# A gated feed-forward kernel: the closing addition of the gate moved from GpSimd to VectorE

## The chip, the cores and the metric

The kernel runs on one core of a Trainium2 chip. The metric is the time of one execution on the device in microseconds, as the median of several runs. The engines are called as in the profile: PE (TensorE), DVE (VectorE), ACT (ScalarE), POOL (GpSimd), SP (SyncE, which issues the DMAs).

## The reference

For each of 8 batches of 512 rows and 512 columns, with FF = 2048:

```python
scale = cond @ norm_w.T + 1.0
ms = jnp.mean(x * x, axis=-1, keepdims=True)
h = x * (scale[:, None, :] * jax.lax.rsqrt(ms + EPS))
u = h @ up_w.T
val, gate = jnp.split(u, 2, axis=-1)
h = val * jax.nn.gelu(gate, approximate=False)
hq = act_quant(h)        # round(h * 127 / max|h| of the row), clipped, scaled back
wq = weight_quant(down_w)  # -1, 0, 1 times a scale from mean|down_w|
y = hq @ wq.T + x
```

## The kernel before

The up-projection is done transposed: features on the partitions, the 512 rows of a batch (T) on the free axis. The 2048 features are cut into 16 slices of 128 (FT = 16). For one slice the value and the gate, each split into two halves of H = 256 rows, are made by seven block products in Winograd's form of Strassen's scheme instead of eight. Each product is six matmuls (two halves of the contraction; the operands are split into a high and a low float16 part and three of the four combinations are summed). The stretch in which PE makes the seven products of slice s is called slot s here. PE issues them in the order p1(s), p5(s), p4(s-1), p6(s), p3(s), p2(s), p7(s): p4, which closes the first half of the gate, belongs to the slice before.

PE accumulates in two pairs of banks (A0/A1, B0/B1), which ACT copies out in between ("snapshots"):

- line 571, `snap_u3`: the sum of p1, p6, p7 of slice s, from bank A into the left half of `snapC`; after it PE may add p4(s) to the bank (line 1019 waits for it), and the bank then holds the first half of the gate.
- lines 576 and 584, `snap_p1` and `snap_u2`, into `snapPU`; line 580, `snap_p5`, from bank B into the right half of `snapC`.
- line 475, `gate_second`: the left half of `snapC` plus its right half. This is the second half of the gate. It is the step that the change moves.
- line 589, `gelu_first`, reads bank A; line 594, `gelu_second`, reads `snapC` and waits for `gate_second`.

ACT's queue in slot s is snap_u3(s-1), snap_p1(s), snap_p5(s), gelu_first(s-1), snap_u2(s), gelu_second(s-1), and then a piece of the work for the next batch (`x_ahead`: squares in slots 2 and 3, `x_out` (line 551) in slots 6, 7, 10, 11, `x_high` (line 557) in slots 8, 9, 12, 13).

DVE's queue in slot s of a batch b is, before the change: in slot 1 `quant_scale` (788 to 796) for batch b-1; in slot 4 `rms`; in slot 5 `refine` (693 to 699) and `normalise` (704) for batch b+1; in slots 9, 10, 13, 14 `x_low` (720); in slots 2 to 9 the three steps `q_scale`, `q_round`, `q_clip` (801, 806, 811) that quantise two slices of batch b-1; `staged_out` (826) after each down-projection; then hidden(s-1) (767: value times c times gelu), value(s) (761) and, after slices 1, 5, 8, 11, 14, 15, `largest` (780, 784), which takes the row maximum over the slices since the last. The one in slot 6, after slice 5, reduces four slices. After slice 15 it completes `m`, which PE transposes in slot 1 (line 1043) for `quant_scale`.

PE makes the down-projection of batch b-1 (line 1055, 16 matmuls per tile of 128 rows) after slots 10, 12, 13 and 14 of batch b.

Batches 2 to 6 are one loop body. Batch 0 also prepares the weights: `w_scale` (DVE, 726 to 735) finds the scale of slice s+2 in slot s, `w_mix` (POOL, 456 to 468) forms the combinations of its blocks, PE transposes them in slot s+1 (983), ACT and DVE write their high and low parts (567 and 741) into `wslots`; slices from 4 on are stored to DRAM and read back in every later batch. Batch 1 also rounds `down_w` (`down_clip` on POOL, 493 and 496; `down_round` on DVE, 848). POOL's queue in later batches holds the addition, `rsqrt` in slot 4 (448) and `x_mix` in slots 8 and 12 (482 to 487).

All order is written by hand, with one semaphore per kind of step; each engine works through its queue in order.

```python
            def gelu_second(b, s):
                act.wait_ge(gate2_ready, FT * b + (s + 1))
...
            def p4(b, s):
                pe.wait_ge(u3_snap, FT * b + (s + 1))
```

Of the kernel before, what the change touches and what calls it, by code (L numbers as in the profile page):

```python
# [23 lines left out]
def gated_ffn_program(nc, x, cond, norm_w, up_w, down_w, out):  # L24
# [4 lines left out]
    B, T, D = x.shape  # L29
# [80 lines left out]
    with ctx:  # L110
# [324 lines left out]
        @block.gpsimd  # L435
        def _(pool):
            pool.memset(ident[:, :], 0.0).then_inc(ident_steps, 1)
            pool.memset(ones[:, :], 1.0)
            pool.memset(neg_half[:, :], -0.5)
            pool.wait_ge(ident_steps, 1)  # L440
            pool.affine_select(out=ident[:, :], in_=ident[:, :], compare_op=ALU.not_equal, fill=1.0,
                               base=0, pattern=[[-1, P]], channel_multiplier=1).then_inc(ident_steps, 1)
            pool.wait_ge(ident_steps, 2)
            pool.tensor_copy(ident16[:, :], ident[:, :]).then_inc(consts_ready, 1)

            def rsqrt(b):
                pool.wait_ge(ms_ready, b + 1)
                pool.tensor_tensor(r_pow[:, :], ms[:, :], neg_half[:, :], ALU.pow).then_inc(pow_ready, 1)

            def w_mix(p):  # L450
                f = wf(p)
                done = MIX * p
                pool.wait_ge(w_scale_ready, p + 1)
                if p >= 2:
                    pool.wait_ge(wT_psum, NC * (p - 1))
                pool.tensor_scalar(f[:, A21:A22 + 1, :].rearrange("p a n -> p (a n)"), wst[:, p % WSTAGE, 1, :],
                                   inv_w[:, VG * p + 1:VG * p + 2], 1.0, ALU.mult, ALU.mult).then_inc(mix_steps, 1)
                pool.tensor_scalar(f[:, A11:A12 + 1:A12 - A11, :],
                                   wst[:, p % WSTAGE, 0, :].rearrange("p (a n) -> p a n", a=2),
                                   inv_w[:, VG * p:VG * p + 1], 1.0, ALU.mult, ALU.mult).then_inc(mix_steps, 1)  # L460
                pool.wait_ge(mix_steps, done + 1)
                pool.tensor_tensor(f[:, S1, :], f[:, A21, :], f[:, A22, :], ALU.add).then_inc(mix_steps, 1)
                pool.wait_ge(mix_steps, done + 2)
                pool.tensor_tensor(f[:, S3, :], f[:, A11, :], f[:, A21, :], ALU.subtract).then_inc(mix_steps, 1)
                pool.wait_ge(mix_steps, done + 3)
                pool.tensor_tensor(f[:, S2, :], f[:, S1, :], f[:, A11, :], ALU.subtract).then_inc(mix_steps, 1)
                pool.wait_ge(mix_steps, done + 5)
                pool.tensor_tensor(f[:, S4, :], f[:, A12, :], f[:, S2, :], ALU.subtract).then_inc(mix_steps, 1)

            def gate_second(b, s):  # L470

                n = FT * b + (s + 1)
                pool.wait_ge(u3_snap, n)
                pool.wait_ge(p5_snap, n)
                pool.tensor_tensor(snapC[:, s % 2, 0:H], snapC[:, s % 2, 0:H], snapC[:, s % 2, H:T], ALU.add)\  # L475
                    .then_inc(gate2_ready, 1)

            def x_mix(b, kp):
                f = xf_of(b, kp).rearrange("p (a t) -> p a t", a=NB)
                done = 8 * b + 4 * kp  # L480
                pool.wait_ge(xf_ready, KT * b + (2 * kp + 2))
                pool.tensor_tensor(f[:, T3, :], f[:, B22, :], f[:, B12, :], ALU.subtract).then_inc(xmix_steps, 1)
                pool.tensor_tensor(f[:, T1, :], f[:, B12, :], f[:, B11, :], ALU.subtract).then_inc(xmix_steps, 1)
                pool.wait_ge(xmix_steps, done + 2)
                pool.tensor_tensor(f[:, T2, :], f[:, B22, :], f[:, T1, :], ALU.subtract).then_inc(xmix_steps, 1)
                pool.wait_ge(xmix_steps, done + 3)
                pool.tensor_tensor(f[:, T4, :], f[:, B21, :], f[:, T2, :], ALU.subtract).then_inc(xmix_steps, 1)

            def down_clip(i):

                pool.wait_ge(dw_loaded[i % 2], 16 * (PIECES // 2 + i // 2 + 1))
                pool.wait_ge(dw_scale_ready, 1)
                pool.tensor_scalar(dwb[:, i % 2, :], dwb[:, i % 2, :], sw[:, 0:1], MAGIC, ALU.mult, ALU.add)\
                    .then_inc(dw_added, 1)
                pool.wait_ge(dw_added, i + 1)
                pool.tensor_scalar(dwb[:, i % 2, :], dwb[:, i % 2, :], MAGIC + 1.0, MAGIC - 1.0, ALU.min, ALU.max)\
                    .then_inc(dw_clipped, 1)

            def batch(b, first=False, final=False):
                for s in range(FT):  # L500
                    gate_second(b if s else b - 1, (s - 1) % FT)
                    if not final:
                        if s == RMS_AT:
                            rsqrt(b + 1)
                        if s in XMIX_AT:
                            x_mix(b + 1, XMIX_AT[s])
                    if first and s in DW_CLIP:
                        down_clip(DW_CLIP[s])

            w_mix(0)  # L510
            rsqrt(0)
            w_mix(1)
            for s in range(FT):
                if s > 0:
                    gate_second(0, s - 1)
                if s + 2 < FT:
                    w_mix(s + 2)
                if s == RMS_AT:
                    rsqrt(1)
                if s in XMIX_AT:  # L520
                    x_mix(1, XMIX_AT[s])
            batch(1, first=True)
            with pool.Fori(2, LAST) as b:
                batch(b)
            batch(LAST, final=True)
            gate_second(LAST, FT - 1)

        @block.scalar
        def _(act):
# [156 lines left out]
        def _(dve):  # L686
# [62 lines left out]
            def c_later():  # L749
                c_rest = c_all[:, FT * VC:B * FT * VC].rearrange("p (b n v) -> p b n v", b=LAST, v=VC)  # L750
                for v, of in enumerate((0, 1, 1)):
                    dve.tensor_tensor(c_rest[:, :, :, v],
                                      c_w[:, of:FT * VG:VG].unsqueeze(1).to_broadcast([P, LAST, FT]),
                                      c_b[:, 1:B].unsqueeze(2).to_broadcast([P, LAST, FT]), ALU.mult).then_inc(c_ready, 1)

            def value(b, s):

                n = FT * b + (s + 1)
                dve.wait_ge(val_psum, n)
                dve.wait_ge(u2_snap, n)  # L760
                dve.tensor_tensor(h_tile(b, s), BB[s % 2][:, :], snapPU[:, s % 2, :], ALU.add).then_inc(val_ready, 1)  # L761

            def hidden(b, s):
                n = FT * b + (s + 1)
                dve.wait_ge(gelu2_done, n)
                dve.wait_ge(val_ready, n)
                dve.scalar_tensor_tensor(out=h_tile(b, s), in0=h_tile(b, s), scalar=c_of(b, s, 0), in1=g[:, s % 2, :],  # L767
                                         op0=ALU.mult, op1=ALU.mult).then_inc(h_ready, 1)
# [80 lines left out]

            def batch(b, first=False, final=False):  # L850
                for s in range(FT):
                    if s == 1:
                        quant_scale(b - 1)
                        if first:
                            dve.wait_ge(dw_steps, 3)
                    if not final:
                        if s == RMS_AT:
                            rms(b + 1)
                        if s == REFINE_AT:
                            refine(b + 1)  # L860
                            normalise(b + 1)
                        if s in XLO_AT:
                            x_low(b + 1, *divmod(XLO_AT[s], 2), XLO_AT[s] + 1)
                    if 0 <= s - QUANT_FROM < PAIRS:
                        q_scale(b - 1, s - QUANT_FROM)
                        q_round(b - 1, s - QUANT_FROM)
                        q_clip(b - 1, s - QUANT_FROM)
                    if not final and s - 1 in DOWN_AFTER:
                        staged_out(b - 1, DOWN_AFTER[s - 1])
                    of, before = (b, s - 1) if s else (b - 1, FT - 1)  # L870
                    hidden(of, before)
                    value(b, s)
                    largest(of, before)
                    if first and s in DW_TERN:
                        down_round(DW_TERN[s])
# [40 lines left out]

            for s in range(FT):
                if s > 0:
                    value(0, s - 1)
                    if s + 2 < FT:  # L920
                        w_scale(s + 2)
# [21 lines left out]
            with dve.Fori(2, LAST) as b:  # L943
                batch(b)
            batch(LAST, final=True)
            hidden(LAST, FT - 1)
            largest(LAST, FT - 1)
            quant_scale(LAST)
# [246 lines left out]
```

## Time and profile before

| | us |
|---|---|
| median of 3 runs | 823.17 (820.63 to 823.93) |
| the profiled execution | 822.39 |
| its span | 820.6 |
| PE busy | 770.3 |
| DVE busy | 616.1 |
| ACT busy | 428.6 |
| POOL busy | 250.9 |
| the moved addition (line 475), 128 times | 101.1 in sum, 0.79 mean |

The granted TensorE clock over the span is 0.989 of full speed. PE's rows name matmuls by line and operand; a matmul of the up-projection lasts 0.27 us in the records and the next starts 0.11 us later, since they are pipelined. The same holds on DVE and ACT to a lesser degree: an independent next instruction starts up to 0.1 us before the recorded end of the one before. In a timeline the columns are the start, the duration, the engine, the line, the operation with what it writes and reads, and, in brackets, the idle time before it with the step that ended it.

### The profile page before, as it was taken

The numbers are of one execution on the slowest core, as the hardware profiler recorded it, in microseconds if no ns is written. First come the engines' busy times: TensorE is split into PE (matmuls) and PEld (weight loads), VectorE is DVE, ScalarE is ACT, GpSimd is POOL, SyncE is SP. The second block draws the span as 40 slices with busy tenths as digits, with TensorE's granted clock in tenths as the row PEclk, the third lists the DMA queues.
The fourth block names the chain that finished last, engine by engine and source line by source line (L and its number), as shares of the span: only waits on it lengthen the run. The fifth ranks groups of instructions, "written<-read, shape, count | busy, mean of one in ns | idle before, by whom it ended". The sixth has DMA issues, their size and how long they took to land.

```text
span 820.6 us, 17515 instructions
## 1 busy us (share of the span) xinstructions
PE 770.3 (94%) x6385; PEld 636.2 (78%) x6385; DVE 616.1 (75%) x890; ACT 428.6 (52%) x997; POOL 250.9 (31%) x313
## 2 busy tenths in 40 slices
PE   5788887987999999999999999999999999999987
PEld 4677776875778897789878887789868987888853
DVE  5889798889854896389846895489657994589577
ACT  4677565564544664355543654355535654445523
POOL 4477777343421232112221232123211232111100
PEclk9999999999999999999999999999999999999999
DMA  4546662745455255443456154535545245505512
GB/s 142 208 133 205 192 213 119 295 156 166 177 184 184 65 197 182 136 173 134 149 179 228 53 194 142 187 114 179 170 163 179 94 175 185 186 32 195 187 52 77
DMA packets 34507, 130.88 MB, mean 159 GB/s; under 512 B 3224, under 2 KB 3744, under 8 KB 34464
## 3 DMA queue, kind: packets, MB, share of 16 engines
q1 hardware_dynamic: 34448, 130.30, 47.1%
q8 instruction: 27, 0.44, 0.2%
q14 instruction: 16, 0.13, 0.1%
q10 hardware_dynamic: 16, 0.00, 0.0%
HBM read 110.89 MB, written 19.40 MB: 159 GB/s over the span
## 4 chain that ended last, share of the span: by engine, by line
PE 73%; DVE 5%; DMA 2%; issue 1%; POOL 1%; ACT 1%; SPq 0%; DVEq 0%; POOLq 0%; ACTq 0%
PE A L1003 11%; PE A L1006 11%; PE A L1005 11%; PE Y L1055 11%; PE B L1006 8%; PE B L1003 8%; PE B L1005 8%; DMA xin<-in_x_dram 2%; DVE h L801 1%; PE X L971 1%; DMA dwb<-in_L_cond_down_w_dram 1%; PE X L1043 1%; DVE h L816 0%; DVE mpart L780 0%; DVE wst L848 0%
## 5 line engine op out<-in xcount | busy, mean ns | idle before, releaser
L1003 PE MATMUL A<-xT,wslots 128*128 (+1 forms) x1024 | 282.2, 276 | 14.8 <-ACT snapC L571 8.5
L1005 PE MATMUL A<-xT,wslots 128*128 (+1 forms) x1024 | 282.2, 276 | 0.0
L1006 PE MATMUL A<-xT,wslots 128*128 (+1 forms) x1024 | 282.1, 275 | 0.0
L475 POOL TENSOR_TENSOR snapC<-snapC 128x256 f32<-128x256 f32 x128 | 101.1, 790 | 463.5 <-ACT snapC L571 462.9
L1005 PE MATMUL B<-xT,wslots 128*128 (+1 forms) x768 | 210.2, 274 | 0.0
L1003 PE MATMUL B<-xT,wslots 128*128 (+1 forms) x768 | 210.2, 274 | 0.0
L1006 PE MATMUL B<-xT,wslots 128*128 (+1 forms) x768 | 210.2, 274 | 0.0
L767 DVE SCALAR_TENSOR_TENSOR h<-h,c_all,g 128x512 f32<-128x512 f32 (+1 forms) x128 | 108.3, 846 | 118.7 <-ACT g L594 117.9
L1003 PEld LDWEIGHTS A<-xT,wslots 128*128 128x128 f16 x1024 | 101.2, 99 | 30.9 <-ACT snapC L571 9.8
L1005 PEld LDWEIGHTS A<-xT,wslots 128*128 128x128 f16 x1024 | 101.2, 99 | 15.1
L1006 PEld LDWEIGHTS A<-xT,wslots 128*128 128x128 f16 x1024 | 101.3, 99 | 12.7
L1055 PE MATMUL Y<-dT,q 128*128 128x512 f16 x448 | 101.3, 379 | 2.1 <-DVE wst L826 2.1
L576 ACT ACTIVATE snapPU<-A 128x256 f32<-128x256 f32 x128 | 49.2, 384 | 97.4 <-PE A L1006 97.4
L571 ACT ACTIVATE snapC<-A 128x256 f32<-128x256 f32 x128 | 49.0, 383 | 95.0 <-PE A L1006 94.9
L761 DVE TENSOR_TENSOR h<-B,snapPU 128x512 f32<-128x512 f32 (+1 forms) x128 | 87.4, 683 | 1.2 <-PE B L1006 1.0
L589 ACT ACTIVATE g<-A,c_all 128x256 f32<-128x256 f32 x128 | 60.6, 473 | 46.7 <-PE A L1006 42.8
L1006 PEld LDWEIGHTS B<-xT,wslots 128*128 128x128 f16 x768 | 75.5, 98 | 9.0
L1005 PEld LDWEIGHTS B<-xT,wslots 128*128 128x128 f16 x768 | 75.5, 98 | 8.8
L1003 PEld LDWEIGHTS B<-xT,wslots 128*128 128x128 f16 x768 | 75.5, 98 | 8.4
L1055 PEld LDWEIGHTS Y<-dT,q 128*128 128x128 f16 x448 | 43.8, 98 | 49.1 <-issue 2.3
L780 DVE TENSOR_REDUCE mpart<-h 128x512 f32<-128x1536 f32 (+2 forms) x40 | 81.0, 2025 | 0.2
L801 DVE TENSOR_TENSOR h<-h,S 128x1024 f32<-128x1024 f32 x64 | 77.5, 1211 | 0.7 <-PE S L1049 0.7
(128 smaller groups left out, 920.1 us busy)
## 6 DMA issues: line engine op xcount, KB each, us to landing
wslots<-w_scratch SPq DMA_DIRECT2D x84, 896.0 KB, 4.7
w_scratch<-wslots SPq DMA_DIRECT2D x12, 896.0 KB, 4.6
wst<-in_L_cond_up_w_dram SPq DMA_DIRECT2D x16, 512.0 KB, 6.2
xin<-in_x_dram SPq DMA_DIRECT2D x8, 1024.0 KB, 7.3
dwb<-in_L_cond_down_w_dram SPq DMA_DIRECT2D x16, 512.0 KB, 4.5
wst<-in_x_dram SPq DMA_DIRECT2D x28, 256.0 KB, 5.4
out_dram<-wst SPq DMA_DIRECT2D x28, 256.0 KB, 5.2
xin<-in_x_dram SPq DMA_DIRECT2D x4, 256.0 KB, 5.1
```

What stands on the lines that cost most here:

```text
L475: pool.tensor_tensor(snapC[:, s % 2, 0:H], snapC[:, s % 2, 0:H], snapC[:, s % 2, H:T], ALU.add)\
L571: act.activation(snapC[:, s % 2, 0:H], BA[s % 2][:, 0:H], ACT.Copy).then_inc(u3_snap, 1)
L576: act.activation(snapPU[:, s % 2, 0:H], BA[s % 2][:, 0:H], ACT.Copy).then_inc(p1_snap, 1)
L589: act.activation(g[:, s % 2, 0:H], BA[s % 2][:, 0:H], ACT.Gelu, scale=c_of(b, s, 1))\
L761: dve.tensor_tensor(h_tile(b, s), BB[s % 2][:, :], snapPU[:, s % 2, :], ALU.add).then_inc(val_ready, 1)
L767: dve.scalar_tensor_tensor(out=h_tile(b, s), in0=h_tile(b, s), scalar=c_of(b, s, 0), in1=g[:, s % 2, :], op0=ALU.mult, op1=ALU.mult).then_ ...
L780: dve.tensor_reduce(into[:, :], h_tiles(b, first, n).rearrange("p n t -> p t n"), AX.X, ALU.max, apply_absolute_value=True).then_inc(max_r ...
L801: dve.tensor_tensor(pair, pair, S[:, :].unsqueeze(1).to_broadcast([P, 2, T]), ALU.mult)\
L1003: pe.matmul(into, high, xh, start=(start and kp == 0), stop=False, skip_group_check=not start)
L1005: pe.matmul(into, high, xl, start=False, stop=False, skip_group_check=not start)
L1006: mm = pe.matmul(into, low, xh, start=False, stop=last, skip_group_check=not start)
L1055: mm = pe.matmul(bank[:, :], of[:, s * T + t * P:s * T + (t + 1) * P], dT[:, s, :], start=(s == first), stop=(s == last))
```

## The change

The additions leave POOL's queue and stand in DVE's. In slot s, gate_second(s-1) is now the first thing in DVE's queue, ahead of everything listed above; in batch 0 it stands ahead of value(s-1) and w_scale(s+2). It waits for the same two snapshots and signals the same semaphore. Nothing else changes.

```diff
-            def gate_second(b, s):
-
-                n = FT * b + (s + 1)
-                pool.wait_ge(u3_snap, n)
-                pool.wait_ge(p5_snap, n)
-                pool.tensor_tensor(snapC[:, s % 2, 0:H], snapC[:, s % 2, 0:H], snapC[:, s % 2, H:T], ALU.add)\
-                    .then_inc(gate2_ready, 1)
-
...
                 for s in range(FT):
-                    gate_second(b if s else b - 1, (s - 1) % FT)
                     if not final:
...
             for s in range(FT):
-                if s > 0:
-                    gate_second(0, s - 1)
                 if s + 2 < FT:
...
             batch(LAST, final=True)
-            gate_second(LAST, FT - 1)
 
...
+            def gate_second(b, s):
+
+                n = FT * b + (s + 1)
+                dve.wait_ge(u3_snap, n)
+                dve.wait_ge(p5_snap, n)
+                dve.tensor_tensor(snapC[:, s % 2, 0:H], snapC[:, s % 2, 0:H], snapC[:, s % 2, H:T], ALU.add)\
+                    .then_inc(gate2_ready, 1)
+
...
                 for s in range(FT):
+                    gate_second(b if s else b - 1, (s - 1) % FT)
                     if s == 1:
                         quant_scale(b - 1)
...
                 if s > 0:
+                    gate_second(0, s - 1)
                     value(0, s - 1)
                     if s + 2 < FT:
                         w_scale(s + 2)
...
             batch(LAST, final=True)
+            gate_second(LAST, FT - 1)
             hidden(LAST, FT - 1)
```

DVE's queue in the loop body (batches 2 to 6), from hidden(5) in slot 6 to value(7) in slot 7, before:

```order
L767 SCALAR_TENSOR_TENSOR h<-h,c_all,g 128x512
L759 REGISTER_ALU
L761 TENSOR_TENSOR h<-B,snapPU 128x512 [waits u2_snap,val_psum]
L780 TENSOR_REDUCE mpart<-h 128x512 [waits h_ready]
L783 ISA
L784 TENSOR_TENSOR m<-m,mpart 128x512 [waits max_ready]
L801 TENSOR_TENSOR h<-h,S 128x1024 [waits qscale_psum]
```

and with the change, where the same steps have the lines 763, 757, 776, 780 and 797:

```order
L763 SCALAR_TENSOR_TENSOR h<-h,c_all,g 128x512
L755 REGISTER_ALU
L757 TENSOR_TENSOR h<-B,snapPU 128x512 [waits u2_snap,val_psum]
L776 TENSOR_REDUCE mpart<-h 128x512 [waits h_ready]
L779 ISA
L780 TENSOR_TENSOR m<-m,mpart 128x512 [waits max_ready]
L749 TENSOR_TENSOR snapC<-snapC 128x256 [waits p5_snap,u3_snap]
L797 TENSOR_TENSOR h<-h,S 128x1024 [waits qscale_psum]
```

The addition (line 749) stands behind the reduction over four slices and its maximum, and ahead of q_scale.

DVE's queue in batch 0, from the last low parts of a slice's weights to the scale of a later slice, before:

```order
L741 TENSOR_TENSOR wslots<-S,wslots 128x256 [waits whi_ready]
L761 TENSOR_TENSOR h<-B,snapPU 128x512 [waits u2_snap,val_psum]
L726 TENSOR_REDUCE inv_w<-wst 128x2 [waits w_loaded2]
L729 TENSOR_SCALAR c_w<-inv_w 128x2 [waits w_steps]
L732 TENSOR_SCALAR c_w<-c_w 128x2 [waits w_steps]
L735 RECIPROCAL inv_w<-c_w 128x2 [waits w_steps]
```

and with the change:

```order
L729 TENSOR_TENSOR wslots<-S,wslots 128x256 [waits whi_ready]
L749 TENSOR_TENSOR snapC<-snapC 128x256 [waits p5_snap,u3_snap]
L757 TENSOR_TENSOR h<-B,snapPU 128x512 [waits u2_snap,val_psum]
L714 TENSOR_REDUCE inv_w<-wst 128x2 [waits w_loaded2]
L717 TENSOR_SCALAR c_w<-inv_w 128x2 [waits w_steps]
L720 TENSOR_SCALAR c_w<-c_w 128x2 [waits w_steps]
L723 RECIPROCAL inv_w<-c_w 128x2 [waits w_steps]
```

The addition stands ahead of value and of the four steps of w_scale.

## Rows read from the trace of the kernel before

**Rows 1.** The page: busy us of each engine, share of the span, instructions

```profile
PE 770.3 (94%) x6385; PEld 636.2 (78%) x6385; DVE 616.1 (75%) x890; ACT 428.6 (52%) x997; POOL 250.9 (31%) x313
```

**Rows 2.** Busy us by stretch: PE, PEld, DVE, ACT, POOL, then clock, DMA share, GB/s

```profile
356.00:446.00 90.00, 89.98 (x760) 74.58 (x760) 66.24 (x90) 46.44 (x112) 20.44 (x25) 1.00 0.47 157
373.00:389.00 16.00, 16.00 (x149) 14.43 (x147) 15.69 (x23) 8.94 (x22) 2.81 (x4) 1.00 0.49 172
```

**Rows 3.** The waits: who waited for whom, us in total, times, longest

```profile
POOL snapC L475 <- ACT snapC L571: 462.9, 112, 7.8
...
ACT g L594 <- POOL snapC L475: 3.8, 3, 2.0
```

**Rows 4.** Timeline of DVE in the prologue: additions of the moved one's shape

```profile
19.46 1.02 DVE L709 TENSOR_TENSOR xf<-xf 128x256 f32<-128x256 f32 x1
20.40 0.94 DVE L710 TENSOR_TENSOR xf<-xf 128x256 f32<-128x256 f32 x1
...
22.59 0.42 DVE L709 TENSOR_TENSOR h<-h 128x256 f32<-128x256 f32 x1
22.92 0.42 DVE L710 TENSOR_TENSOR h<-h 128x256 f32<-128x256 f32 x1
```

**Rows 5.** Timeline of DVE, slots 5 to 7 of a steady batch

```profile
373.75 0.15 DVE L693 TENSOR_TENSOR r_a<-r_pow 128x4 f32<-128x4 f32 x1
...
378.87 1.22 DVE L767 SCALAR_TENSOR_TENSOR h<-h,c_all,g 128x512 f32<-128x512 f32 x1
...
382.92 0.75 DVE L767 SCALAR_TENSOR_TENSOR h<-h,c_all,g 128x512 f32<-128x512 f32 x1
...
384.18 3.73 DVE L780 TENSOR_REDUCE mpart<-h 128x512 f32<-128x2048 f32 x1
387.95 0.69 DVE L784 TENSOR_TENSOR m<-m,mpart 128x512 f32<-128x512 f32 x1
388.56 1.21 DVE L801 TENSOR_TENSOR h<-h,S 128x1024 f32<-128x1024 f32 x1
```

**Rows 6.** Timeline of POOL, ACT and PE in the same slots and slot 8

```profile
373.98 0.72 POOL L475 TENSOR_TENSOR snapC<-snapC 128x256 f32<-128x256 f32 x1 [2.62 <-ACT snapC L571]
378.57 0.97 POOL L475 TENSOR_TENSOR snapC<-snapC 128x256 f32<-128x256 f32 x1 [3.86 <-ACT snapC L571]
383.59 0.73 POOL L475 TENSOR_TENSOR snapC<-snapC 128x256 f32<-128x256 f32 x1 [4.05 <-ACT snapC L571]
...
386.03 0.50 ACT L594 ACTIVATE g<-snapC,c_all 128x256 f32<-128x256 f32 x1
386.43 0.68 ACT L551 ACTIVATE xf<-X,scl 128x512 f32<-128x512 f32 x1
388.15 0.38 ACT L571 ACTIVATE snapC<-A 128x256 f32<-128x256 f32 x1 [1.04 <-PE A L1006]
...
389.26 0.27 PE L1003 MATMUL A<-xT,wslots 128*128 x1
```

**Rows 7.** Timeline of DVE, ACT and PE at the turn to the next batch

```profile
441.68 0.69 DVE L784 TENSOR_TENSOR m<-m,mpart 128x512 f32<-128x512 f32 x1
445.07 0.77 DVE L784 TENSOR_TENSOR m<-m,mpart 128x512 f32<-128x512 f32 x1
...
442.42 0.50 ACT L594 ACTIVATE g<-snapC,c_all 128x256 f32<-128x256 f32 x1
...
446.07 0.65 PE L1043 MATMUL X<-ident,m 128*128 128x128 f32 x4
```

**Rows 8.** The waits of batch 0, and one row of POOL in batch 1

```profile
POOL q L456 <- DVE inv_w L735: 40.7, 16, 8.5
...
PE S L983 <- POOL q L468: 8.8, 5, 3.0
...
PE Y L983 <- POOL q L468: 6.1, 5, 2.1
...
208.56 1.04 POOL L475 TENSOR_TENSOR snapC<-snapC 128x256 f32<-128x256 f32 x1
```

## The prediction

> **What bounds the kernel now.** I read the busy times first. PE is busy 94% of the span, DVE 75%, POOL 31% [rows 1]. One batch in the middle of the run, 356 to 446 us, shows PE busy 89.98 of 90 us; there every microsecond that is added must be a wait of PE, since no matmul changes. In the same batch DVE is busy 66.2 us, so it has 24 us of idle time; but the 16 us from 373 to 389 have DVE busy 15.7 of 16 [rows 2]. The spare time of DVE lies in other slots. So the question is not whether 16 more additions fit into a batch, but who waits while DVE is behind.
>
> The waits say what the addition costs on POOL today: nothing. POOL sits idle 463 us in total before it, waiting for ScalarE's snapshot, and ScalarE's second gelu waited for POOL only 3.8 us in the whole run [rows 3].
>
> Names: gate(s) is the moved addition for slice s. It runs in slot s+1, the stretch in which PE makes the seven products of slice s+1; q stands for the three quantising steps that DVE does in slots 2 to 9, hidden(s), value(s) and largest(s) for lines 767, 761 and 780 with 784.
>
> **The price of one addition.** Before the change it lasts 0.73 us on POOL [rows 6]. The same shape, 128x256 float32 from SBUF, stands on DVE in the prologue: 0.42 us long, the next independent instruction 0.33 us after it [rows 4]. I take 0.34 of DVE's time and 0.42 until its result is out. The upper end is the first such row, 1.02 us, taken while POOL was working on SBUF too [rows 4]; the lower end is the 0.33. The result is thus 0.3 us younger than now if DVE is free to start. The Trainium skill (GPSIMD Engine Reference, section 4.1, Engine selection) gives elementwise work to VectorE and calls GpSimd about 2x slower for two inputs. The trace agrees on the duration (0.73 to 0.42); by that rule alone every second gelu is sooner, PE's waits stay as they are, and the time is at most today's. [...]
>
> **The change, step by step.** 128 additions leave POOL, 128 go into DVE's in-order queue at the head of each slot: behind value(s) and largest(s-1), and ahead of q, hidden and the rest. So an addition now waits for whatever DVE is behind with, and DVE waits for the snapshot before it may go on to q.
>
> *Batches 2 to 6, slots 5 to 8.* Before, DVE is done with value(4) and starts slot 5's first step at 373.75 [rows 5]. The snapshot for gate(4) is ready at 373.98, when POOL started it [rows 6]. So the next step starts at 373.98 + 0.34 = 374.32, 0.57 later. In exchange hidden(4), at 378.87, gets shorter: it took 1.22 us while POOL's gate(5) ran beside it (0.97 us instead of 0.73), and takes 0.75 undisturbed [rows 5, 6], so 0.47 come back. gate(5) adds 0.34. value(6) and largest(5) follow; the reduction alone is 3.73 us, and DVE reaches the next step at 388.56 today [rows 5], then at 388.56 + 0.57 - 0.47 + 0.34 = 389.00. That is where gate(6) now starts; POOL started it at 383.59 [rows 6]. Result at 389.42, gelu at 389.50. ScalarE's gelu was at 386.03, then x_out at 386.43, then the next snapshot (line 571) at 388.15 after idling [rows 6]. Now gelu 389.50, x_out 0.40 later (the spacing of those rows) at 389.90, the snapshot 0.58 after that (0.68 less the same overlap) at 390.48, done 0.38 later at 390.86. PE's product p4(7) in slot 8 must have this snapshot; its first matmul was at 389.26 [rows 6], now about 390.91. **PE waits 1.65 us**, in each of batches 2 to 6: 8.25 us. gate(1), gate(2) and gate(3) fall into idle time of DVE or push it by less than it has. Once PE has lost 1.65 us, DVE has won as much, so I expect no second stall in slots 9 and 10; from slot 11 on four stretches of down-projection give DVE time.
>
> Both ends of this term: zero if DVE were 1.65 us less behind; with 0.94 us per addition (the spacing of the first prologue rows, [rows 4]) instead of 0.34, the three that count, gate(4) to gate(6), add 1.8, so 3.45 us a batch, 17.3 in all.
>
> *Batch 7* has neither refine and normalise nor x_out in these slots, so DVE is less behind: 0.3 us, between 0 and 1.65.
>
> *The turn of the batch, slot 0.* largest(14) ends with the step at 441.68, whose successor may start 0.61 later, at 442.29. gate(15) now starts there, and its result is seen by the gelu at 442.29 + 0.42 + 0.08 = 442.79, which ran at 442.42 [rows 7]: 0.37 later. hidden(15), value(0) and largest(15) follow without a gap until 445.84, and PE's transposes of m start at 446.07 [rows 7], so they wait for it already. The 0.37 goes straight onto PE, at the seven turns and once more in the tail: 8 x 0.37 = 3.0 us. Ends: 0 and 8 x 0.8.
>
> *Batch 0.* Here a loop runs through w_scale on DVE, w_mix on POOL and the transposes on PE. POOL waited for DVE's inv_w ahead of all 16 w_mix, and PE waited ten times for POOL's last step, 14.9 us together [rows 8]. The addition on POOL was therefore free, and on DVE it stands in front of w_scale and delays it by 0.34. The loop spans two slots (slice s+2 is mixed in slot s and transposed in slot s+1), so what it is too long is shared by two slots: 7 x 0.34 = 2.4 us. Ends: 0 and 15 x 0.42 = 6.3.
>
> *Batch 1.* DVE is behind with q and the rounding of down_w. Three additions (1.0) come before the rounding that PE waits for, 0.47 of contention goes, and POOL's addition at 208.56 (1.04 us, ahead of x_mix, [rows 8]) goes too; part of this is hidden behind loads of down_w. I take +0.5; ends -1.0 and +2.5.
>
> **Sum:** 8.25 + 0.3 + 3.0 + 2.4 + 0.5 = 14.45 us. The profiled execution took 822.39 us, so 836.8; the median of the runs is 0.8 above it, so **837.6 us** in terms of the median.
>
> **The rivals.**
> - *The stall behind largest(5) is absorbed* (DVE is less behind than I add up, or ScalarE has slack that I don't see). Only batch 0, batch 1 and the turns cost: 823.2 + 3.0 + 2.4 + 0.5 = 829.1. For it: all of the 1.65 rests on adding up starts to a tenth. Against: gate(6) moves by 5.4 us, and ScalarE's idle time between x_out and the snapshot is about 1.1 us.
> - *Each addition costs what it does beside a busy POOL.* 17.3 + 1.5 (batch 7) + 3.0 + 6.6 (seven of 0.94) + 2.5 = 30.9, so 854. Against: POOL is busy 20.4 of 90 us in a steady batch [rows 2], 11.7 of them (16 of 0.73) the additions themselves.
> - *Faster: the two engines stop holding each other up.* gate(5) and hidden(4) lengthened one another by 0.24 and 0.47. If the additions always found DVE free, the 3.8 us of gelus waiting for POOL [rows 3] and the 1.04 ahead of x_mix in batch 1 [rows 8] would go: 823.2 - 4.8 = 818.4. It decides if DVE is less than 1 us behind at the head of each slot; at slot 7 it is over 5 behind [rows 5, 6], which speaks against it. The Trainium skill (SBUF — State Buffer, Who interferes with whom) has such a rule: a DVE instruction with two SBUF inputs and a GpSimd one that reads SBUF exclude each other. The overlap of gate(5) and hidden(4) agrees with it.
> - *The change does nothing:* excluded, since the order of the instructions shows the additions on DVE.
>
> **Chances.** My forecast 0.62, absorbed 0.17, dear additions 0.13, faster 0.06, several stalls per batch above all that 0.02. A measurement of this kernel can tell about 0.5% (4.1 us) from nothing. Slower by more than that: 0.62 + 0.12 (of 0.17, as some of it lies below 827.3) + 0.13 + 0.02 = 0.89. Within: 0.05 + 0.02 = 0.07. Faster: 0.04. The forecast's own ends are some 832 and 843; the range goes down to 827 to take in most of the absorbed case and up to 850 for part of the dear one, which leaves out a little under 2 in 10.
>
> **What would show it.** In a steady batch, one wait of PE at p4 of slot 8 for line 571's snapshot, 1 to 2 us long, five times; the gelu of slice 6 about 3.5 us later in its slot; the transposes of m 0.4 us later. The addition on DVE about 0.42 us long, hidden(4) back at 0.75. A batch should take 92.0 us instead of 90.0. I am wrong if PE shows no wait in slot 8, if it waits in several slots of a batch, or if batch 0 grows by over 6 us.

## The result, and the profile after

| us | before | after |
|---|---|---|
| median of 4 runs | 823.55 (820.63 to 824.24) | 834.11 (832.48 to 835.72) |
| the profiled execution | 822.39 | 833.67 |
| its span | 820.6 | 831.8 |

The kernel takes 1.0138 times as long with the change, 95% interval 1.0116 to 1.0160. It is 10.6 us slower in the medians and 11.3 between the two profiled executions; the forecast was 14.4.

The page's busy line of the kernel after, which answers to [rows 1]:

```profile
PE 773.7 (93%) x6385; PEld 635.8 (76%) x6385; DVE 650.5 (78%) x1018; ACT 428.1 (51%) x997; POOL 151.6 (18%) x185
```

POOL lost 99 us of work and DVE gained 34. Neither explains 11 us. PE has the same matmuls; of the 11.2 us of its span 7.8 are idle time and 3.4 busy time, 0.9 of these in batch 1 and 1.7 behind the last transpose of m, at a granted TensorE clock of 0.95 in both where it was 0.97 and 0.99. PE transposes `m` once per batch (line 1043 before, 1042 after), and the starts of these transposes cut the run into stretches that can be compared one by one. Before they start at 158.87, 265.98, 356.02, 446.07, 536.12, 626.16, 716.03 and 789.61; after at 163.63, 268.17, 360.00, 451.68, 543.37, 635.03, 726.26 and 800.71.

| stretch, from one transpose of m to the next | before | after | difference | forecast |
|---|---|---|---|---|
| start to m of batch 0 | 158.87 | 163.63 | +4.76 | +2.77 (2.4 and one turn) |
| m of batch 0 to m of batch 1 | 107.11 | 104.54 | -2.57 | +0.87 (0.5 and one turn) |
| the next five, to m of batch 6 | 450.05 | 458.09 | +8.04 | +10.1 (8.25 and five turns) |
| to m of batch 7 | 73.58 | 74.45 | +0.87 | +0.67 (0.3 and the tail's 0.37) |
| the rest | 30.99 | 31.09 | +0.10 | 0 |

A stretch in the middle, 360.00 to 451.68, takes 91.68 us where it took 90.05. The granted TensorE clock is 1.00 in both, so the clock has no part in this difference. All waits of PE between 268 and 720 us in the kernel after (columns: engine, line, what it waited for: us in total, times, longest us); in the kernel before there is none:

```profile
PE A L1002 <- ACT snapC L559: 5.5, 5, 1.2
PE X L1042 <- DVE m L780: 2.0, 5, 0.4
```

Those are the predicted places: p4 in slot 8 and the turn of the batch, five times each. The surroundings of both in one batch, from the timeline of the kernel after:

```profile
388.13 3.72 DVE L776 TENSOR_REDUCE mpart<-h 128x512 f32<-128x2048 f32 x1
...
391.88 0.69 DVE L780 TENSOR_TENSOR m<-m,mpart 128x512 f32<-128x512 f32 x1
392.49 0.42 DVE L749 TENSOR_TENSOR snapC<-snapC 128x256 f32<-128x256 f32 x1
393.05 0.51 ACT L582 ACTIVATE g<-snapC,c_all 128x256 f32<-128x256 f32 x1 [2.94 <-DVE snapC L749]
393.46 0.67 ACT L539 ACTIVATE xf<-X,scl 128x512 f32<-128x512 f32 x1
394.03 0.37 ACT L559 ACTIVATE snapC<-A 128x256 f32<-128x256 f32 x1
394.46 0.28 PE L1002 MATMUL A<-xT,wslots 128*128 x1 [1.06 <-ACT snapC L559]
...
447.50 0.42 DVE L749 TENSOR_TENSOR snapC<-snapC 128x256 f32<-128x256 f32 x1
...
448.73 0.75 DVE L763 SCALAR_TENSOR_TENSOR h<-h,c_all,g 128x512 f32<-128x512 f32 x1 [0.82 <-ACT g L582]
...
450.71 0.69 DVE L780 TENSOR_TENSOR m<-m,mpart 128x512 f32<-128x512 f32 x1
...
451.68 0.54 PE L1042 MATMUL X<-ident,m 128*128 128x128 f32 x3 [0.44 <-DVE m L780]
```

Read it from the top: the reduction over four slices, the maximum behind it, then gate(6), then in ACT's queue the gelu, x_out and the next snapshot, and last PE's p4, which waited for that snapshot. ACT's gelu was idle 2.94 us before it; the snapshot that PE needs stands two places behind. PE's idle time reads 1.06 because it is counted from the modelled end of the matmul before; from start to start it is 1.33 where two independent matmuls stand 0.11 apart, so the wait costs about 1.22 us. At the turn of the batch (the last four rows) the transposes of m wait 0.44 by the row, 0.40 more than before. 1.22 and 0.40 are 1.62 of the 1.64 us per batch.

### The profile page after: what moved, and what is told of

Same layout as the page of the kernel before. It is cut to its first block, busy times and chain, and to the rows that moved or that the text cites. A ratio compares the mean times of both kernels' runs of the same rounds, so it can differ in the third digit from the quotient of the medians.

```text
span 831.8 us, 17435 instructions
## 1 busy us (share of the span) xinstructions
PE 773.7 (93%) x6385; PEld 635.8 (76%) x6385; DVE 650.5 (78%) x1018; ACT 428.1 (51%) x997; POOL 151.6 (18%) x185
## 4 chain that ended last, share of the span: by engine, by line
PE 60%; DVE 15%; issue 6%; ACT 1%; POOL 1%; DVEq 1%; ACTq 0%
PE Y L1054 11%; PE A L1002 9%; PE A L1005 9%; PE A L1004 9%; PE B L1005 6%; PE B L1004 6%; PE B L1002 6%; DVE mpart L776 5%; DVE h L797 2%; DVE h L757 1%; DVE q L802 1%; DVE snapC L749 1%; DVE xin L692 1%; PE A L1054 1%; PE B L1054 1%
## 5 line engine op out<-in xcount | busy, mean ns | idle before, releaser
L1002 PE MATMUL A<-xT,wslots 128*128 (+1 forms) x1024 | 281.0, 274 | 18.1 <-ACT snapC L559 12.1
L763 DVE SCALAR_TENSOR_TENSOR h<-h,c_all,g 128x512 f32<-128x512 f32 (+1 forms) x128 | 101.2, 790 | 97.9 <-ACT g L582 96.5
L582 ACT ACTIVATE g<-snapC,c_all 128x256 f32<-128x256 f32 x128 | 64.2, 502 | 57.2 <-DVE snapC L749 57.1
```

Of the source, the lines that this page charges most:

```text
L582: act.activation(g[:, s % 2, H:T], snapC[:, s % 2, 0:H], ACT.Gelu, scale=c_of(b, s, 2))\
L1002: pe.matmul(into, high, xh, start=(start and kp == 0), stop=False, skip_group_check=not start)
```

## The experiments

Lines 559 and 571 are the same snapshot, 1002 and 1003 the same matmul of p4; in kernels that keep both versions of `gate_second` the lines are some 16 higher. "Steady batch" is the stretch from one transpose of m to the next in batches 2 to 5: 90.04 before, 91.68 after. Where a diff says POOL or DVE, the addition of that slice is issued by that engine, at the place that it has in the kernel before or after.

**Which additions cost: slices 6 and 15 put back (e1), and those two alone moved (e2).**

```diff
 # e1: the kernel after, but
+    DVE_LATER = tuple(s for s in range(FT) if s not in (6, 15))   # batches 1 to 7; the other two on POOL
 # e2: the kernel before, but
+    DVE_LATER = (6, 15)                                           # batches 1 to 7; all others on POOL
```

> Everything as in the changed kernel, but from batch 1 on the additions of slices 6 and 15 go back to GpSimd (14 of 16 stay on VectorE). Theory 'place': PE waits only where the addition stands behind a maximum over several slices that is still running, so both waits of a steady batch (1.22 us at p4 of slot 8, 0.40 us at the transposes of m) vanish; a steady batch takes 90.0 to 90.1 us instead of 91.7, and the time falls by 5 x 1.62 plus about 1.3 for batches 1 and 7: 824 to 825.5. Rival 'load': what costs is VectorE's added work, whatever the slice; 14/16 of the cost stays, a steady batch takes 91.5 us and the time is about 832.7.

> The kernel before, but from batch 1 on the additions of slices 6 and 15, and only these, are on VectorE. Place: both waits are there with only 2 of 16 additions moved; a steady batch takes 91.6 to 91.7 us, the time is 823.5 + 5 x 1.6 + 1 to 2 = 832.5 to 833.5. Load: 2/16 of 1.65 us per batch, about 825.

Measured: e1 829.04 us (828.28 to 830.87), 1.0073 times the kernel before (1.0049 to 1.0097), steady batch 90.55. e2 832.79 us (830.01 to 834.25), ratio 1.0106 (1.0070 to 1.0141), steady batch 91.68 to 91.69. The waits of PE in e2 between 268 and 724 us:

```profile
PE A L1018 <- ACT snapC L574: 5.5, 5, 1.1
PE X L1058 <- DVE m L796: 1.6, 4, 0.4
```

Two additions of sixteen cost a steady batch all that the sixteen cost, as the theory of the place had it, and e2's time is the expected one. e1 came out neither way: its steady batch was expected at 90.0 to 90.1 (place) or 91.5 (load), and its time is 3.5 us above the upper end for the place. So the 14 others by themselves are not free: without the stall behind the maximum, a smaller one appears in the next slot. The timeline of e1:

```profile
395.83 0.75 DVE L779 SCALAR_TENSOR_TENSOR h<-h,c_all,g 128x512 f32<-128x512 f32 x1
396.50 0.68 DVE L773 TENSOR_TENSOR h<-B,snapPU 128x512 f32<-128x512 f32 x1
397.10 0.42 DVE L765 TENSOR_TENSOR snapC<-snapC 128x256 f32<-128x256 f32 x1
...
397.65 0.51 ACT L597 ACTIVATE g<-snapC,c_all 128x256 f32<-128x256 f32 x1 [2.13 <-DVE snapC L765]
398.06 0.83 ACT L560 ACTIVATE xT<-xf 128x768 f32 x1
...
398.80 0.36 ACT L574 ACTIVATE snapC<-A 128x256 f32<-128x256 f32 x1
...
399.22 0.28 PE L1018 MATMUL A<-xT,wslots 128*128 x1 [0.40 <-ACT snapC L574]
```

It is the same pattern one slot later: gate(7) behind value(7), the gelu idle for 2.13 us, x_high, the snapshot, p4(8). In the kernel after gate(7) also stands there and the gelu is idle for 1.48 us before 397.84, but PE doesn't wait, since it has just lost 1.22 us that DVE has won.

**Another place in the same queue: ahead of the maximum (e3), and two finer placements (e6, e10).**

```diff
 # e3: the kernel after, but in batches 1 to 7; DVE, slot s
-                    gate_second(b if s else b - 1, (s - 1) % FT)
...
                     value(b, s)
+                    gate_second(b, s)
                     largest(of, before)
...
```

> All additions on VectorE as in the changed kernel, but from batch 1 on the addition of slice s stands ahead of the maximum (largest) in slot s instead of behind it. Place: a steady batch takes 90.0 to 90.2 us although VectorE does all 16 additions; the time is 824 to 826, what is left being batch 0. Load: no difference from the changed kernel, 834.

Measured: 833.70 us (831.50 to 836.13), ratio 1.0125 (1.0088 to 1.0161), steady batch 91.06 against 91.68. The expectation for the place (90.0 to 90.2, 824 to 826) was missed, and the time is hardly below that of the change; what the steady batches gave, the start and batch 1 took back (m of batch 0 at 164.92, batch 1 106.43 us). The stall of slot 8 is gone, but not the cost: PE waits 0.41 us at p4(8), as in e1, and 0.47 at the turn. There gate(0) stands ahead of the maximum of slice 15 and waits for a snapshot, and so holds up m. The timeline of e3 at the turn:

```profile
450.75 0.68 DVE L757 TENSOR_TENSOR h<-B,snapPU 128x512 f32 x1
451.09 0.38 ACT L559 ACTIVATE snapC<-A 128x256 f32<-128x256 f32 x1 [1.19 <-PE A L1005]
451.51 0.43 DVE L749 TENSOR_TENSOR snapC<-snapC 128x256 f32<-128x256 f32 x1
...
451.85 0.68 DVE L776 TENSOR_REDUCE mpart<-h 128x512 f32<-128x512 f32 x1
...
453.49 0.65 PE L1042 MATMUL X<-ident,m 128*128 128x128 f32 x4 [0.47 <-DVE m L780]
```

So a place can be too early as well as too late. In e6 batch 0 is on POOL, gate(0) goes behind the maximum, and gate(7) to the head of its own slot:

```diff
 # e6: batch 0 on POOL; DVE, batches 1 to 7, slot s
                     if s == 1:
+                        gate_second(b, 0)
                         quant_scale(b - 1)
+                    if s == 7:
+                        gate_second(b, 7)      # head of the slot
                         if first:
                             dve.wait_ge(dw_steps, 3)
...
                     value(b, s)
+                    if s not in (0, 7):
+                        gate_second(b, s)
                     largest(of, before)
```

> Batch 0's additions on GpSimd, all later ones on VectorE, but each at a place where VectorE reaches it in time: slice 7's at the head of slot 7, slice 0's behind the maximum that closes m, all others ahead of the maximum of their slot. Place: a steady batch takes 90.0 to 90.2 us with all 16 additions on VectorE (up to 90.4 if slice 7's place makes value(7) late); the time is 822 to 825. Load: 91.0 us or more, since two earlier changes of place still left 0.5 and 1.0 us.

Measured: 836.76 us (836.34 to 837.55), ratio 1.0175 (1.0147 to 1.0202), where 822 to 825 was expected, though the steady batch fell to 90.53. Two things happened. In the steady batches the wait moved on once more, 0.35 us now at p4 of the slot after (gate(8) behind value(8)). And batch 1 took 117.6 us instead of 107.1: DVE waits 12.7 us for snapshots, 4.7 of them at the head of slot 7, where gate(7) now stands ahead of its own input, and the rounding of down_w, which PE waits for, stands behind. e3 has the additions in their own slots too, but not gate(7) at the head of slot 7; there the same wait is 3.5 us in batch 1. (The edit also moved DVE's wait for `dw_steps` from slot 1 to slot 7 of batch 1. What it waits for is a step of DVE's own that is over by 155.8, ahead of value(15), so it holds nothing up at either place.) The waits of e6 from 160 to 278 us:

```profile
DVE snapC L765 <- ACT snapC L574: 12.7, 11, 4.7
...
PE Y L1010 <- DVE wst L860: 12.5, 4, 4.0
```

The second wait is 6.1 in the kernel before. The waits are only half of the loss. The windows of batch 1, before and in e6 (columns as in [rows 2]), have PE idle for 9.5 and 14.7 us, and for the same matmuls busy for 97.64 and 102.94 us, at a granted clock of 0.97 and 0.91:

```profile
158.87:265.98 107.11, 97.64 (x825) 79.76 (x825) 78.17 (x98) 53.47 (x119) 37.13 (x39) 0.97 0.54 184
160.44:278.04 117.60, 102.94 (x824) 82.47 (x825) 83.32 (x115) 53.70 (x119) 22.69 (x22) 0.91 0.49 166
```

e10 puts these right: batch 0 and slice 6 of batch 1 stay on POOL, the rest of batch 1 is at the slot's head as in the change (but for slice 15, which is ahead of the maximum in slot 15), and in batches 2 to 7 gate(8) stands ahead of hidden(7).

```diff
 # e10, DVE, slot s
+                    if s and (first or s == 1):   gate_second(b, s - 1)   # head of the slot
+                    if s == 7 and not first:      gate_second(b, 7)       # head of the slot
...
+                    if s == 8 and not first:      gate_second(b, 8)       # ahead of hidden
                     hidden(of, before)
                     value(b, s)
+                    if s == FT - 1 or not (first or s in (0, 7, 8)):
+                        gate_second(b, s)
                     largest(of, before)
```

> Batch 0 and slice 6 of batch 1 on GpSimd, all other additions on VectorE: in batch 1 at the head of the slot, from batch 2 on ahead of the slot's maximum, with slice 0 behind it, slice 7 at the head of slot 7 and slice 8 ahead of hidden(7). Place: a steady batch takes 90.0 to 90.15 us with all 16 additions on VectorE; the time is that of the run with only batch 1's additions moved, 821 to 823. Load: VectorE cannot do 16 more additions in this batch without a wait of PE; 90.4 us or more, 824 or more.

Measured: 822.35 us (821.11 to 823.54, 12 runs) against 823.24, ratio 0.9990 (0.9979 to 1.0002). Steady batch 90.26. Its window of one batch, which answers to the first of [rows 2]:

```profile
356.00:446.26 90.26, 90.18 (x762) 74.43 (x761) 70.65 (x107) 46.47 (x112) 7.31 (x9) 1.00 0.48 157
```

DVE does all sixteen additions there and is busy 70.65 us where it was 66.2, and PE is busy 90.18 of 90.26. Between 268 and 720 us no wait of a matmul is listed. The place in the timeline of e10:

```profile
383.52 0.69 DVE L773 TENSOR_TENSOR h<-B,snapPU 128x512 f32<-128x512 f32 x1
...
384.12 0.42 DVE L765 TENSOR_TENSOR snapC<-snapC 128x256 f32<-128x256 f32 x1
...
384.45 3.73 DVE L792 TENSOR_REDUCE mpart<-h 128x512 f32<-128x2048 f32 x1
...
386.00 0.50 ACT L597 ACTIVATE g<-snapC,c_all 128x256 f32<-128x256 f32 x1
```

gate(6) starts at 384.12, ahead of the reduction, and the gelu has no wait. The same 16 additions on the same engine cost 0.2 us per batch here (90.0 to 90.15 was expected) and 1.64 in the change: what the steady batches lose is the place, not the load.

**Does DVE's lateness reach PE in full? (e8)** In batches 1 to 7 one more addition of 128x256 stands behind gate(4) and one behind gate(5); what they write is used by nothing.

```diff
                     .then_inc(gate2_ready, 1)
+                if s in (4, 5) and not is_first(b):
+                    dve.tensor_tensor(mpart[:, 0:H], ones, ones, ALU.add)   # ones repeated to 256
```

> The changed kernel with one more addition of 128x256 float32 on VectorE behind each of the additions of slices 4 and 5 from batch 1 on (its result is used nowhere). Place: VectorE reaches slice 6's addition 0.67 us later, and PE's wait at p4 of slot 8 grows by that from 1.22 to 1.9 us; a steady batch takes 92.3 to 92.4 us, the time is 834.1 + 5 x 0.67 + 0.5 = 838. If VectorE had slack ahead of that point, nothing changes: 834.

Measured: 838.82 us (838.18 to 839.05), ratio 1.0196 (1.0169 to 1.0223); steady batch 92.35, 0.67 more than the change, as expected. Two additions of 0.34, the step from one DVE instruction to the next, are 0.68. PE's wait at p4(7) grew from 5.5 to 8.6 us in five batches:

```profile
PE A L1007 <- ACT snapC L559: 8.6, 5, 1.7
```

These 0.67 us of DVE's time ahead of the critical place went to PE in full; it is the one size that was tried.

**The two ends of the run: only batch 0 moved (e4), all but batch 0 moved (e5), batch 1 alone (e7).**

```diff
 # e4: the kernel before, with batch 0's additions on DVE
 # e5: the kernel after, with batch 0's additions on POOL
 # e7: the kernel before, with batch 1's additions on DVE, without slices 6 and 15
```

> Only the 16 additions of batch 0 are on VectorE, the rest on GpSimd. Chain theory: in batch 0 the transposes wait 3.3 us longer in sum for w_mix and the turn to batch 1 about 1.4 us more, so the transposes of m in batch 1 come about 4.8 us later than at 158.87; of this some 2.3 us is got back in batch 1, where the load of x for batch 2 held up the kernel before: time 823.5 + 2 to 3 = 825.5 to 826.5. Rival: the 2.6 us that batch 1 got back came from its own additions leaving GpSimd; then nothing is got back here and the time is 828.3.

> Batch 0's additions on GpSimd as before, all later ones on VectorE. Theory 'batch 1 gains' (the addition no longer stands in GpSimd's queue behind the clipping of down_w, which waits for its loads): the stretch from the transposes of m in batch 1 to those in batch 2 takes about 104.5 us instead of 107.1, a steady batch 91.7, and the time is 823.6 - 2.5 + 8.2 + 1.3 = 830.6. Theory 'hidden delay' (batch 1 only got back what batch 0 had lost, since the load of x had more time): the stretch takes 107.1 or more and the time is 833.1 or more.

> Only batch 1's additions are on VectorE, without slices 6 and 15; all others on GpSimd. Batch 1 gains: the stretch from the m of batch 1 to that of batch 2 takes 104 to 104.8 us, steady batches 90.04, and the time is 821 (820.3 to 821.8), faster than the kernel before. Hidden delay: no difference from the kernel before, 823.6.

Measured: e4 827.63 us (826.12 to 828.32), ratio 1.0045 (1.0027 to 1.0064), m of batch 0 at 164.22, steady batch 90.08. e5 832.39 us (829.00 to 832.96), ratio 1.0111 (1.0080 to 1.0143), steady batch 91.8. Both times lie between the two that were expected. The two excesses, 3.9 and 9.5 us against the medians of the kernel before that were taken with them (823.72 and 822.85), are 13.4 together where the whole change cost 10.6. Most of the missing 2.8 us is in batch 1: it takes 107.11 before, 107.04 in e4, 106.74 in e5, and 104.54 with both. Two waits of PE are a part of it. In the timeline of before:

```profile
171.37 0.40 PE L1003 MATMUL A<-xT,wslots 128*128 128x256 f16 x1 [2.34 <-ACT snapC L571]
...
213.73 0.28 PE L1003 MATMUL A<-xT,wslots 128*128 128x256 f16 x1 [1.02 <-ACT snapC L571]
```

of e4:

```profile
175.78 0.28 PE L1018 MATMUL A<-xT,wslots 128*128 128x256 f16 x1 [1.53 <-ACT snapC L574]
...
217.08 0.39 PE L1018 MATMUL A<-xT,wslots 128*128 128x256 f16 x1 [2.48 <-ACT snapC L574]
```

and of e5, which has the first alone:

```profile
171.59 0.40 PE L1018 MATMUL A<-xT,wslots 128*128 128x256 f16 x1 [2.22 <-ACT snapC L574]
```

The first wait is behind ACT's queue, where the squares of x for the next batch stand ahead of the snapshot; in the kernel before they start at 168.80, idle for 2.68 us until the load of x that was issued at 155.00 is there. The wait is 2.1 to 2.3 us in the six kernels with batch 0 on POOL and 0.9 to 1.5 in e1, e4 and e9; it is gone only in the kernel after, e3 and e8. These three are also the only ones whose granted clock falls to 0.50, the lower of TensorE's two levels, from 2 to 4 us behind the transposes of m, ahead of which PE had been idle for 2.0 us. (e1, idle for 2.2 us there, kept 1.00, so the wait alone doesn't decide it.) The first six us behind the transposes, before and after:

```profile
158.87:164.87 6.00, 6.00 (x54) 5.30 (x55) 5.20 (x10) 2.11 (x6) 2.66 (x3) 1.00 1.01 417
163.63:169.63 6.00, 6.00 (x40) 4.92 (x41) 3.81 (x10) 1.16 (x3) 0.00 (x0) 0.72 1.01 406
```

PE makes 40 matmuls after and 54 before. A matmul that starts 3.00 us behind the transposes before (161.87) starts 4.53 behind after (168.16). So PE was slower there, and the load was in when ACT came to it. The p4 that had waited stands 12.50 us behind the transposes before and 11.53 after (175.16): what the vanished wait is worth is 1.0 us, not 2.3.

The second wait is in slot 9, where POOL had the addition between the clipping of down_w and x_mix (the 1.04 us of [rows 8]); e4 keeps the addition there and waits 2.48, while e5, e7 and the kernel after, which have moved it, do not wait there. The addition isn't all of it: e1 has moved this one too and waits 1.36 (217.67), since POOL's clipping, which starts when the load of down_w is in (211.32), is later there.

e7 tests the gain of batch 1 by itself: 821.46 us (819.17 to 825.38, 12 runs), ratio 0.9992 (0.9972 to 1.0011). Batch 1 takes 105.93 us in its profile, where 104 to 104.8 was expected; the 1.02 is gone, the load's 2.1 has stayed. The gain of 1.2 us stands in one trace and is too small for the runs to show.

**How batch 0 loses (e9).** As e4, but the addition stands behind value and w_scale.

```diff
                 if s > 0:
-                    gate_second(0, s - 1)
                     value(0, s - 1)
                     if s + 2 < FT:
                         w_scale(s + 2)
+                    gate_second(0, s - 1)
```

> As the run with only batch 0's additions on VectorE, but there the addition stands behind value(s-1) and w_scale(s+2) instead of ahead of them. Chain theory (what batch 0 costs is the delay of w_scale, on which w_mix and the transposes hang): the transposes of m in batch 1 come at 158.9 to 160.5 us instead of 164.2, and the time is 823 to 825. Rival: the cost is VectorE's total work in batch 0 (0.34 us in each slot of an engine that is busy over 80% there) or its contention with w_mix; then they still come at 163 or later, and the time stays at 827.5.

Measured: 825.06 us (823.82 to 827.08, 10 runs), ratio 1.0021 (1.0007 to 1.0036). The last `inv_w` of batch 0, on which POOL's mixing and then PE's transposes hang, starts at:

| | last inv_w | m of batch 0 |
|---|---|---|
| batch 0 on POOL: before, e2, e5, e6, e7, e10 | 136.29, 136.43, 136.22, 137.47, 135.95, 136.81 | 158.87, 158.89, 159.35, 160.44, 158.80, 160.14 |
| on DVE ahead of value: after, e4, e1, e3, e8 | 139.62, 140.61, 141.51, 140.82, 141.09 | 163.63, 164.22, 165.76, 164.92, 165.17 |
| on DVE behind w_scale: e9 | 138.19 | 162.10 |

The row of the kernel after that answers to the one of before at 136.29:

```profile
139.62 0.17 DVE L723 RECIPROCAL inv_w<-c_w 128x2 f32<-128x2 f32 x1
```

In the means of these profiles batch 0 loses 4.2 us up to the last inv_w and 5.3 up to m; e9 lies in the middle, 1.7 and 2.7 above the row of POOL, and so between what the two theories expected. By the medians it is 1.8 us above the kernel before where e4 is 3.9, with intervals that overlap.

The chain itself shows in PE's waits up to 158 us. PE waits for POOL's last mixing step (two lines of waits, summed) 10.1 to 12.1 us in the six kernels of the first row, 14.5 to 15.2 in the five of the second, and 12.7 in e9. So ahead of w_scale the addition lengthens this wait by about 3 us (12.0 to 15.2 between before and after), and behind w_scale by 0.7. What e9 has in its place is a longer wait for the snapshot (6.6 against 5.2 before) and for DVE's low parts (1.3 against 0.4). How much of the whole loss of batch 0 the chain is, these profiles can't say: PE's idle time from 25 us to m is 18.9 to 20.5 us in the first row, 22.5 to 24.7 in the second and 23.2 in e9, and its busy time for the same matmuls differs by 2.9 us within the second row alone (114.0 in the kernel after at a granted clock of 0.98, 116.9 in e8 at 0.92). Some additions are longer beside POOL's mixing, as these rows of the kernel after show:

```profile
144.46 0.72 POOL L468 TENSOR_TENSOR q<-q 128x256 f32<-128x256 f32 x1
144.55 0.91 DVE L749 TENSOR_TENSOR snapC<-snapC 128x256 f32<-128x256 f32 x1
```

## Why the prediction came out as it did

**Direction, range and the deciding place were right.** The stall at p4(7) in slot 8, behind the four-slice reduction, is there five times, and apart from the turns PE waits nowhere else in the steady batches; a turn costs 0.40 against 0.37; the addition lasts 0.42 and hidden(4) is back at 0.75; 2.94 us of idle gelu stand where "about 3.5 us later" was forecast. The reading that carried it, 15.7 busy us in the 16 from 373 to 389 [rows 2] rather than 75% of the span, is confirmed by e2 (two additions carry it all), e10 (elsewhere in the queue they cost 0.2) and e8 (0.67 us more ahead of it are 0.67 us more of PE).

**The 1.65 was 1.22: the step on the relief was too small.** The prediction gave hidden(4) 0.47 us back and thought of no other step. There is one, in the timeline of before, beside POOL's gate(4):

```profile
374.13 0.60 DVE L697 TENSOR_SCALAR r_a<-r_b 128x4 f32<-128x4 f32 x1
```

and after, at the same place of the batch:

```profile
378.64 0.17 DVE L685 TENSOR_SCALAR r_a<-r_b 128x4 f32<-128x4 f32 x1
```

That is another 0.43, and 1.65 less 0.43 is 1.22. Relief (0.47 and 0.43) thus cancels the load of gate(4) and gate(5) (0.57 and 0.34): with the start of the stretch as zero, 360.00 after and 356.02 before, DVE gets past the maximum at 392.49 - 3.98 = 388.51, and at 388.56 before. DVE is no later than it was. The whole 1.22 is that gate(6) now stands there, when POOL had started it at 383.59 [rows 6]. Five such terms are 6.1 instead of 8.25; this accounts for the 8.04 against 10.1.

**Batch 0's 2.4 was too small.** The step "7 x 0.34" took one delay per two slots. PE's waits for POOL's mixing grew by 3.2 us, and the last inv_w came 3.3 us later in the profile after and 4.2 in the mean; then the turn to batch 1 added another 1.4 where 0.37 stood:

```profile
163.63 0.63 PE L1042 MATMUL X<-ident,m 128*128 128x128 f32 x4 [1.98 <-issue]
```

It read 0.54 before. The end named for "I am wrong" (6 us) wasn't reached. The row puts no engine to this wait, but it is DVE's way to m. From the start of value(15) to the end of m's last step DVE takes 4.26 us before and 5.69 after, and in all twelve profiles this time less PE's wait is 3.70 to 3.72 us. The rows of the kernel after on this way:

```profile
158.44 0.99 DVE L749 TENSOR_TENSOR snapC<-snapC 128x256 f32<-128x256 f32 x1
...
159.47 0.51 ACT L582 ACTIVATE g<-snapC,c_all 128x256 f32<-128x256 f32 x1 [1.32 <-DVE snapC L749]
...
162.10 1.43 DVE L780 TENSOR_TENSOR m<-m,mpart 128x512 f32<-128x512 f32 x1
```

It is the pattern of the turn that the prediction had, with gate(15) now behind the mean of down_w and value(15), and made longer because POOL clips down_w at that time: gate(15) takes 0.99 instead of 0.42, so that hidden(15) starts 2.17 us behind value(15) instead of 0.79; hidden(15) gives 0.34 back, and m's last step takes 1.43 instead of 1.03. That is the 1.4. The prediction had taken this turn for one like the others.

**Batch 1's +0.5 had the wrong sign.** Its terms took the 1.04 of POOL's queue as a gain, rightly, but no step looked at PE's wait of 2.34 us at 171.37, which was in the trace of before and stands behind the load of x, nor at the clock. The -2.57 is made of 3.49 us less idle time of PE (9.47 to 5.98) and 0.92 more busy time for the same matmuls, at a granted clock of 0.95 instead of 0.97. The idle time lost the 2.34, the 1.02 and 0.4 of waits for the rounding of down_w, and got 0.30 of a wait for m at the end. Of the kernels with nearly the same queues e1 took 104.08 us for this stretch without the fall of the clock, and e8 105.17 with it, so the gain is 1.9 to 3.0 us and doesn't hang on the clock. It lies beyond the lower end that was given, 1.0.

**Batch 7 and the tail** came to 0.97 against 0.67.

**The sum was 3.2 us too high** (14.45 against 11.3 between profiles): 2.1 too much in the steady batches, 3.4 in batch 1, and 2.3 too little in batch 0, its turn and the end. Part of the nearness is these errors cancelling, and that is luck.

**The rivals.** The absorbed stall is excluded by the five waits. Dear additions are too: the 79 of the steady batches last 421 ns in the mean. The faster case had its mechanism right and its condition wrong: the two engines do free each other (0.90 us per batch), the shorter wait of POOL's queue in batch 1 is real, and with the additions at the best places that were tried (e10, batch 0's on POOL) the kernel still only equals the one before, because in the steady batches PE was busy 89.98 of 90 us and there was nothing to win.

## What to carry to other kernels

Moving a short step to a faster engine puts it behind whatever that in-order queue does there. Before moving it, write down for each slot when the new engine gets to that place and when the result is due; the worst slot sets the price, and here the mean load said nothing. If it must move, choose the place per slot: not behind a long reduction, and not ahead of a step that is due before its own input is there. Once a stall is removed the next latest place shows, so go on until PE has no wait left, and measure the first and second batch apart from the loop, since their queues hold other work.

## What the runs showed of the hardware

- A DVE step over 128x4 elements, 0.17 us by itself, took 0.60 while an addition of two SBUF operands ran on POOL (the row at 374.13), and the median of its 8 instances is 600 ns before and 170 after. A tiny step lost as much as a large one (0.47 on 128x512); that fits a step that waits for the other engine's instruction rather than one that runs more slowly. The Trainium skill (SBUF — State Buffer, Who interferes with whom) says that `tensor_scalar` on DVE can enter a mode that takes the pair of ports shared with GpSimd, and that the other then blocks for a whole instruction. The two durations agree with it; no run here tells the mode apart.
- Moving the addition did not end this. In the change's batch 0, at its end beside the clipping of down_w (0.99 at 158.44), and in e10's slots with x_mix the moved addition itself is the stretched one (0.91 at 144.55, 0.94 at 389.04 in e10), there beside POOL's own additions.
- In the kernel after, e3 and e8 the granted clock fell to 0.50 behind an idle time of PE of 2.0 us at the turn to batch 1; matmuls then started 0.21 us apart instead of 0.11 (from 164.44 to 167.42 in the kernel after). In e1 it stayed at 1.00 behind an idle time of 2.2. In the steady batches, with a wait of 1.1 us each, it stayed at 1.00.
- Five profiles with the same instructions up to the end of batch 0 have its last inv_w between 139.62 and 141.51, at granted clocks of 0.91 to 0.97. A difference under 2 us in that stretch isn't to be read from one profile each; three steady batches of the kernel after, at 1.00, repeat within 0.03 us (91.66 to 91.69).
